# Expert weights held in SBUF from elements 5 and 6 on, and copied into the ring by VectorE

## The reference, cut to what matters

```python
m = _layernorm(x, ln2_g, ln2_b)
xt = m.reshape(-1, Dd)                       # all tokens, 128 channels
probs = jax.nn.softmax(xt @ Wg, axis=-1)     # 8 experts
wts, idx = jax.lax.top_k(probs, 2)
wts = wts / jnp.sum(wts, axis=-1, keepdims=True)
h1 = jax.nn.gelu(jnp.einsum('td,edf->etf', xt, W1) + b1[:, None, :])   # 128 -> 512
ye = jnp.einsum('etf,efd->etd', h1, W2) + b2[:, None, :]               # 512 -> 128
moe_out = jnp.sum(wts[..., None] * ye[idx, jnp.arange(T)[:, None], :], axis=1)
```

## Time and profile before

| | |
|---|---|
| median of three runs | 1007.14 us (1004.87 to 1008.16) |
| the profiled execution | 1008.6 us |
| its span, first to last instruction | 1006.9 us |
| mean granted TensorE clock over the span | 0.894 of full speed |
| TensorE busy with matmuls | 825.8 us, 82% |
| VectorE busy | 663.3 us, 66% |
| ScalarE busy | 599.2 us, 60% |
| GpSimd busy | 416.5 us, 41% |
| packets of the hardware DMA queue, share of 16 engines' span | 33.6% |

### The profile page before, as it was taken

The page is one execution under the profiler, slowest core; times in us unless marked ns, Lnnn a source line. Parts: engine busy times, 40 slices in busy tenths (PEclk is TensorE's granted clock), DMA queues, the critical chain, the costliest instruction groups (busy, mean ns, idle before and its releaser), DMA issues.

```text
span 1006.9 us, 15854 instructions
## 1 busy us (share of the span) xinstructions
PE 825.8 (82%) x5376; PEld 518.8 (52%) x5376; DVE 663.3 (66%) x1341; ACT 599.2 (60%) x1016; POOL 416.5 (41%) x496
## 2 busy tenths in 40 slices
PE   3668998898989998889898989889978887966562
PEld 1535364344556554455565556555645554766552
DVE  5478767978897788788967887878754762231012
ACT  2124546455877884568768876787658766543221
POOL 6535432347424644665344535365540131142323
PEclk9775877899999997989999999999979997996766
DMA  6502313962423200052333210533333205684842
GB/s 195 163 11 76 113 58 129 348 198 68 159 88 97 80 8 6 25 183 93 98 101 105 85 56 29 181 96 105 101 108 93 71 29 181 194 274 155 253 146 78
DMA packets 106285, 116.76 MB, mean 116 GB/s; under 512 B 7983, under 2 KB 89310, under 8 KB 106206
## 3 DMA queue, kind: packets, MB, share of 16 engines
q1 hardware_dynamic: 102110, 107.36, 33.6%
q0 software_dynamic: 4096, 8.40, 2.5%
HBM read 77.24 MB, written 38.49 MB: 115 GB/s over the span
## 4 chain that ended last, share of the span: by engine, by line
PE 42%; DVE 19%; ACT 19%; issue 9%; POOL 5%; another core or an unknown queue 4%; DMA 1%; SPq 1%; POOLq 0%; ACTq 0%; DVEq 0%
PE psV L1177 8%; DVE QA L1460 7%; PE psB L1165 7%; ACT PT L946 5%; ACT H L974 5%; PE psY L1251 5%; PE psA L1241 5%; PE psB L1149 3%; PE psA L1025 3%; PE psA L1093 3%; ACT L974 3%; PE psA L1013 2%; PE psA L1078 2%; ACT L946 1%
## 5 line engine op out<-in xcount | busy, mean ns | idle before, releaser
L1460 DVE TENSOR_REDUCE QA<-psB 128x2 f32<-128x1024 f32 x256 | 312.0, 1219 | 134.1 <-PE psB L1149 119.4
L946 ACT ACTIVATE PT<-psB 128x1024 f32<-128x1024 f32 x256 | 261.8, 1023 | 138.6 <-PE psB L1165 121.2
L1165 PE MATMUL psB<-Q,KT 32*128 32x512 f32 x512 | 134.6, 522 | 40.8 <-ACT PT L946 21.8
L1149 PE MATMUL psB<-KT,Q 24*128 24x512 f32 x512 | 137.2, 530 | 24.8 <-DVE QA L1460 22.6
L1241 PE MATMUL psA<-MX,WB 128*128 128x128 f32 x792 | 109.7, 291 | 51.1 <-ACT H L974 32.6
L1177 PE MATMUL psV<-PT,VA 128*32 128x512 f32 x1024 | 150.4, 662 | 0.4
L974 ACT ACTIVATE H<-psA,WB 128x128 f32<-128x128 f32 x396 | 109.3, 377 | 42.5 <-PE psA L1241 22.9
L1241 PEld LDWEIGHTS psA<-MX,WB 128*128 128x128 f32 x792 | 100.4, 203 | 59.4 <-issue 40.6
L1251 PEld LDWEIGHTS psY<-WB,H 128*128 128x128 f32 x792 | 102.4, 203 | 30.6 <-ACT H L974 17.3
L1251 PE MATMUL psY<-WB,H 128*128 128x128 f32 x792 | 113.5, 293 | 2.1 <-issue 1.8
L1165 PEld LDWEIGHTS psB<-Q,KT 32*128 32x128 f32 x512 | 49.9, 191 | 122.7 <-ACT PT L946 79.1
(11 more groups left out here) (195 smaller groups left out, 1328.3 us busy)
## 6 DMA issues: line engine op xcount, KB each, us to landing
WB<-w_rows SPq DMA_DIRECT2D x99, 578.0 KB
pairs<-XT SPq DMA_DIRECT2D x2, 5120.0 KB, 18.3
outs<-XT SPq DMA_DIRECT2D x2, 5120.0 KB, 33.5
XT<-pairs SPq DMA_DIRECT2D x99, 64.0 KB
outs<-YT SPq DMA_DIRECT2D x99, 64.0 KB
w_rows<-WB SPq DMA_DIRECT2D x8, 578.0 KB, 3.2
X<-in_L_attn_x_dram SPq DMA_DIRECT2D x8, 256.0 KB, 2.9
H<-in_L_ffn_W_dram SPq DMA_DIRECT2D x8, 256.0 KB, 3.9
```

The source lines that it names most:

```text
L946: act.activation(PT[:, (c % 2) * G + j:(c % 2) * G + j + 2, :], psT, ACT.Exp, scale=SCALE).then_inc(t_taken.sem, 1)
L1149: pe.matmul(dst[:, h, :], chunk(Q1[r, g, :], c), KT[r, g, :], start=True, stop=True).then_inc(s_full.sem, 1)
L1165: pe.matmul(psT[:, h, :], chunk(KT[r, g, :], c), Q2[r, g % 2, :], start=True, stop=True).then_inc(t_full.sem, 1)
L1460: dve.tensor_reduce(QA[:, c, g * G + j:g * G + j + 2, RM], plain(b, i), AX_X, ALU.max).then_inc(s_taken.sem, 1)
```

## The change

The new tensor `RW` holds all eight experts' weights and biases (9248 float32 in each partition, 4.7 MB in all). There is no room for it beside the rest, so it lies over fifteen buffers of the head and tail stages (`X`, `Z0`, `XA`, `D`, `MK`, `MV`, `MR`, `K`, `V`, `R`, `PP`, `EE`, `EV`, `AA`, `BB`), which are now pieces of it and are dead once the tail of element 7 is done. SyncE fills it with eight DMAs of 578 KB (`all_weights`), after `x_used` says that this is so. From w21 on `weights_in` issues nothing. In its place VectorE reads the tile's expert from `TMAP` into a register and copies 128x1156 float32 from `RW` into the ring (`copy_weights`), three tiles a window, right after `tile_out` of window w-2. TensorE and ScalarE wait on the count of copies in place of the DMA. The computation is the same.

```diff
+        RW = sb("RW", [P, E, 2 * F + NF + C])
+        RW_FLAT = RW[:, :, :].rearrange("p e n -> p (e n)")
...
-        X = sb("X", [P, NT, C])
-        Z0 = sb("Z0", [P, NT, C])
+        X = early([NT, C])
+        Z0 = early([NT, C])
...
+        RESIDENT = WINDOW_0[GROUPS - 2]
+        COPY_AT = {}
+        for w in range(RESIDENT, sum(WINDOWS)):
+            COPY_AT[w] = max(START[w - 2] + 10, SLOTS * (MEMBERS[window_group(w)][-1] + 1) + 22.5)
...
+        def weights_ready(engine, n):
+            if window(n) >= RESIDENT:
+                engine.wait_ge(w_copied, n - members(RESIDENT)[0] + 1)
+            else:
+                engine.wait_ge(w_in[ring(n)], landed(n))
...
+            def all_weights():
+                sp.wait_ge(x_used.sem, x_used.at(B - 1, 1))
+                for e in range(E):
+                    sp.dma_start(RW[:, e, :], WS[e]).then_inc(experts_in, 16)
+
             def weights_in(w):
+                if w >= RESIDENT:
+                    return
...
+                    if n == B - 2 and s == 24:
+                        all_weights()
...
-                act.wait_ge(w_in[ring(n)], landed(n))
+                weights_ready(act, n)
...
-                pe.wait_ge(w_in[ring(n)], landed(n))
+                weights_ready(pe, n)
...
+            def copy_weights(w):
+                group = window_group(w)
+                if w == RESIDENT:
+                    dve.wait_ge(experts_in, 16 * E)
+                if w == WINDOW_0[group]:
+                    dve.wait_ge(map_ready.sem, map_ready.at(group, 1))
+                dve.wait_ge(y_taken.sem, y_taken.at(w - 2, 1))
+                for n in members(w):
+                    i = within(n)
+                    both = dve.value_load(TMAP[i:i + 1, group % 2:group % 2 + 1], min_val=0, max_val=E * (BLOCKS - 1) - 1)
+                    dve.tensor_copy(WB[:, ring(n), :], RW[:, both & (E - 1), :]).then_inc(w_copied, 1)
...
                         tiles(n, at, TILE)
+                        for w in COPY_AT:
+                            if SLOTS * n + at == COPY_AT[w]:
+                                copy_weights(w)
                         extras(at, *now)
```

More of the change, by code:

```diff
@@ L22 @@
+import math
 from contextlib import ExitStack
@@ L143, in build, with early @@
         col = {n: cols[:, i:i + 1] for i, n in enumerate(VEC)}
-        X = sb("X", [P, NT, C])
-        Z0 = sb("Z0", [P, NT, C])
-        ZA = sb("ZA", [P, NT, C])
[L149 to L161, removed]
+        RW = sb("RW", [P, E, 2 * F + NF + C])
+        RW_FLAT = RW[:, :, :].rearrange("p e n -> p (e n)")
+        used = [0]
+        def early(shape):
+            size = math.prod(shape)
+            used.append(used[-1] + size)
+            flat = RW_FLAT[:, used[-2]:used[-1]]
+            return flat.rearrange("p (a n) -> p a n", n=shape[1]) if len(shape) == 2 else flat
+        X = early([NT, C])
+        Z0 = early([NT, C])
+        ZA = sb("ZA", [P, NT, C])
+        XA = early([T + 1])
+        D = early([T])
+        MK = early([T])
+        MV = early([T])
+        MR = early([T])
+        K = early([T])
+        V = early([T])
+        R = early([T])
+        PP = early([T + 1])
+        EE = early([4, T])
+        EV = early([T])
+        AA = early([T + 1])
+        BB = early([T + 1])
         N2 = K
@@ L372, in build @@
         y_out = [sem(f"y_out_{i}") for i in range(2)]
+        experts_in = sem("experts_in")
+        w_copied = sem("w_copied")
         def group_of(n):
```

## The result

The changed kernel takes 1000.16 us in the median of six runs (996.83 to 1002.12), the kernel before 1006.71 us in six (1004.87 to 1008.16). The ratio is 0.994, with a 95% interval of 0.9913 to 0.9967. The forecast was 986 us, a gain of 21; the gain is 6.5. The sign was right and the time lies in the range; the size was wrong by a factor of three.

What follows compares the result with a forecast made beforehand. It took the last stage to lose 36.2 us over undisturbed windows, mostly to stalls with weights beside GpSimd's requests. Less 27.2 us gained, plus 5.0 for copies, 1008.6 became 986.4, stated as 986 us, range 971 to 1005.

Steps and rivals of the forecast that it cites:

- Where the weights stood in the stalls: Last stage, two stalls of 33.5 us beside GpSimd's request rows: without weights only 4 and 5 us stay.
- w29: Window w29 took 12.5 us beside a queue full of weights; without them it loses 5.3 us, down to 7.2.
- The eight new loads: Loads of RW between w18's weights and rows: cost nothing, hidden by attention; if late, by 2 to 3 us.
- A copy: VectorE's 128x1156 copy from SBUF to SBUF: 0.94 us, a window of three taken at 4 us with register reads.
- Where copies are in the way: Copies of w21, w25 and w26 ahead of score maxima, ZM and SEL: together 5.0 us lost, bounds 0 and 14.
- The 1 us for ZM: Copies of w25 stand before ZM and move it by up to 3.4 us; 1 us charged.
- The sum: Profiled execution: 1008.6 - 27.2 + 5.0 = 986.4 us; median of the runs 1.5 us lower, stated as 986 us.
- the second rival: Last stage: the stalls belong to GpSimd's requests and stay, only w29 gains, 1008 us; chance 0.14.
- The third rival: VectorE's copies hold off GpSimd's requests, stretching rows and stalls by 0.39, 1021 us; chance 0.11.
- The fourth rival: Copies become the bound: VectorE needs 7.8 us a window where TensorE needs 7.2, about 1005 us; chance 0.08.

Runs made afterwards that it cites:

- unfed_6: The kernel before without the weights of w21 and later, no loads and no copies, on a stalled occasion: 1003.67 us against 1006.53 for the kernel before.
- the broken row: The changed kernel with group 3's 16 gathers issued four at a time, on a stalled occasion: 992.44 us against 1006.81 for the kernel before.
- a_busy: The changed kernel with each of group 3's 16 gathers replaced by a GpSimd operation of the same length, stalled occasion: 992.52 us against 1006.53 for the kernel before.
- after_5: The changed kernel, unaltered, measured again on a quiet occasion: 959.0 us against 963.97 for the kernel before, ratio 0.9926.
- before_5: The kernel before, unaltered, measured again on a quiet occasion: 963.91 us, ratio 0.9991.
- a_few: The changed kernel without the 16 gathers of group 3 (elements 5 and 6), quiet occasion: 963.34 us against 963.0 for the kernel before.

## Why the prediction was right or wrong

**Where the weights stood in the stalls: wrong.** The step that failed is "I leave 4 us for the row of 14 requests and 5 for the 16, by the earlier trace rows, out of 33.5". In unfed_6, with neither weights nor copies, the row of 14 costs 13.1 us at w26 (20.3 less 7.2) and the row of 16 costs 17.4 (31.8 less 14.4). Before, with the weights, it was 13.1 and 19.7. (Against the 6.4 us that w26 takes when quiet, the first is 13.9 both times.) What the weights added between these two traces is 2.3 of 33, within their scatter. I had the argument against it in the text, 44 GB/s through the second part of the first stall, and gave it 0.14. What misled me was to carry the 3 to 4 us of the earlier trace rows over to longer rows: the cost is not so much for each request. Sixteen in one row cost 16.0 us, the twelve of the broken row that stand beside windows 1.6.

**w29: right in kind.** 5.3 us were forecast and 5.3 came; quiet it is 7.5.

**The eight new loads: right.** w17 and w18 took 22.3 and 22.8 us after, 23.6 and 22.8 before. They cost nothing.

**A copy: 0.94 us forecast, 763 ns measured**, in the groups of the kernel after:

```profile
L1619 DVE COPY WB<-RW 128x1156 f32 x38 | 29.0, 763 | 13.7 <-DVE YT L1606 9.3 <-issue 3.0
```

With the one read that does not hide, a window of copies is 3.2 us against the 4 I took.

**Where copies are in the way: named right, priced low.** 5.0 us were forecast, 7.9 came (2.8 and 1.3 at w20 and w21, 3.8 at w25). SEL moved by 3.2 us where I had 4, and TensorE waited 1.92 on it where I had 3.1; w25 lost 3.8 all the same. At w20 I let 3.11 us of idle time absorb the copies. That idle time lay beside a row of scatters, and was part of what held the windows up; that nothing is free in it is my reading. The 4.1 us of w20 and w21 are of one pair, and scatter as said above. The 1 us for ZM did not come.

**The sum.** With the stalls that stayed, 1008.6 - 5.3 + 7.9 = 1011 us, the second rival with the dearer copies. The profiled execution had 998.8: 6.7 us less in the stalls and the windows beside them, and 5.7 of early lead, which I take for scatter since the layout gives nothing. How much of the 6.7 is due to the change isn't settled by one pair. The forecast itself had a slip: 986.4 for the profiled execution less 1.5 is 985 for the median, not 986.

**The rivals.** The second held in its mechanism. The rule that TensorE waits on nobody (the Trainium skill, SBUF — State Buffer, "Who interferes with whom") does not cover this case: in unfed_6 its results come 17.9 us late beside GpSimd's requests, and in a_busy, with other work in place of the requests, they are not late. The page speaks of the ports of SBUF, and no run here shows where the results wait. That page's other rule, that DMA does not contend with an engine, agrees with unfed_6, where taking the weights away took no stall away. The third rival's mechanism is there and small:

```profile
899.00 1.59 DVE L1619 COPY WB<-RW 128x1156 f32 x2 [0.19 <-issue]
899.29 1.42 POOL L836 DMA_INDIRECT pairs<-ZM,IDX  x1 [0.30 <-issue]
```

A request that meets a copy takes 1.21 us in the mean of 14 in after_5, the 42 others from 800 us on 0.96. That is the port rule of "SBUF: two separate sides" on the same page, and the trace agrees in kind; but the row of 14 grew only from 16.7 to 17.2 us in the first pair, and from 17.6 to 18.8 with its last request from before_5 to after_5, not by 0.39 of itself. The fourth rival did not come: w30 to w33 stay at 7.20 quiet. Its sum was off too: with the 9 us that it names for the three places it gives 1000 us, and 1005 only with 14.

**What stays open.** Why an occasion is quiet or stalled. Chip 12 was both, so it is not the chip. And by what way a long row of requests delays TensorE's results: in 899 to 915 of the kernel after VectorE was busy for 5.04 us and the queues moved 63 GB/s beside it.

## What to carry to other kernels

When an engine's results come late with no releaser, cut the suspects one at a time before pricing a change on one of them: leave out the transfers, then exchange the requests for other work of the same length. Try breaking up long rows of GpSimd's indirect DMAs beside dense TensorE work, and measure it on occasions of both kinds: it returned 10 to 15 us here on stalled ones and cost 3 to 4 on quiet ones. When a window is sped up, follow the longest chain past it (here SEL, ranks, scatters, rows): what is won inside can be waited out at its end.

## What the hardware showed that I had not expected

- The same kernel takes 963 or 1007 us depending on the occasion, each steady over 6 to 31 runs, and nearly all of the difference lies beside rows of requests: 43.6 between `tile_out` of w33 in two traces of the kernel before (the first and before_5), 1.9 of that before w16, 13.9 at w26 and 19.7 at w30 and w31.
- A row of 16 requests costs TensorE 16.0 us, twelve of them in shorter pieces 1.6; yet beside the row of four at w24 it loses 1.5 to 3.4.
- 128x1156 float32 from SBUF to SBUF take VectorE 763 ns, less for each element than the 417 ns of 128x512.
- A kernel that leaves out the 16 gathers of group 3 takes 4.8 us longer from its last store to its end (a_few against after_5).
